# Rotating the query and key heads: the cosine product of the next vector ahead of the rest part of the one before

## The chip, the cores and the metric

The kernel runs on one core of a Trainium2 chip. The metric is the time of one execution on the device in microseconds (us). A core has five engines that work side by side: TensorE (PE in the profile, with its weight loads as PEld), VectorE (DVE), ScalarE (ACT), GpSimd (POOL) and SyncE (SP), which issues transfers. Each runs its own list of instructions in order and waits on semaphores that the others raise.

## The reference

A feed-forward part, attention and a second feed-forward part, each behind a layer norm and added to x. x has 4 sequences of 512 tokens of 256 values. In the attention, 16 query heads of 128 share 4 key heads. The part that the change touches is the rotation of queries and keys:

```python
def apply_rope(x):
    ...
    cos = jnp.cos(ang).astype(x.dtype)
    sin = jnp.sin(ang).astype(x.dtype)
    x1, x2 = (x[..., :half], x[..., half:])
    return jnp.concatenate([x1 * cos - x2 * sin, x1 * sin + x2 * cos], axis=-1)
...
q = apply_rope(q)
k = apply_rope(k)
...
scores = jnp.einsum('bhqd,bhkd->bhqk', q, k) * scale
causal = jnp.triu(jnp.ones((S, S), dtype=bool), k=1)
scores = jnp.where(causal, -jnp.inf, scores)
attn = jax.nn.softmax(scores, axis=-1)
out = jnp.einsum('bhqk,bhkd->bhqd', attn, v)
```

## The kernel before

**Steps.** The attention runs in 16 steps, one for each pair of key head and sequence. Each step has 4 query heads, so there are 5 vectors to rotate per step, r = 0 (the key) to 4, each 128 x 512 (128 values of a head in the partitions, 512 tokens). While step s computes its scores and outputs, the vectors of step s + 1 are projected and rotated. Steps 1 to 13 are a loop; step 0 is mixed with the end of the first feed-forward part, steps 14 and 15 are written out. Products are kept precise by splitting every operand into a leading part in fp32r and a rest, and multiplying three times.

**One vector's way.** TensorE projects it into the PSUM bank `pj`. ScalarE copies it into `raw[r]` (`raw_out`, L1528, raises `raw_done`). SyncE copies its two halves crosswise into `swap[r]` by two transfers. GpSimd then works on it in `rotate`: L1281 multiplies `raw[r]` by the cosine into `rot[r % 2]`, L1283 multiplies `swap[r]` by the sine, L1285 adds the two (raises `sum_done`). ScalarE copies the sum in fp32r to `qh` or, for r = 0, to the keys (`rotated_lead`, L1502, raises `qh_done`), and GpSimd subtracts that leading part from the sum (`rest`, L1273, raises `ql_done`). There are two buffers `rot`, so the cosine of vector r must come behind the rest of vector r - 2.

**ScalarE's order** in step s, for head h = 0 to 3: two copies of transposed probabilities (`prob_lead`, L1549), two exponentials (L1543), for h = 0 `raw_out(s + 1, 2)`, two more exponentials, for h = 1 and 2 `raw_out(s + 1, h + 2)`, for h = 3 `raw_out(s + 2, 0)` and `(s + 2, 1)`, for h = 0 `rotated_lead(s + 1, 0)` and `(s + 1, 1)` one behind the other, then the third `prob_lead`, the copy of the output (L1553), and for h > 0 `rotated_lead(s + 1, h + 1)`.

**Probabilities.** VectorE finds the row minima of the negated masked scores (L1386), ScalarE takes the exponentials and their sums, VectorE inverts the sums (L1391) and multiplies the probabilities by them in place (`normalise`, L1395): four TENSOR_SCALAR instructions of 128, 256, 384 and 512 columns, in SBUF. TensorE transposes the result (`transpose_p`, L1713). In step s, head h, TensorE computes the scores of the head after next, the transposes of the next head (eight, then two), and the output of head h (L1727 to L1729); in between stand the projections (L1648 to L1650) and the output projection of the step before (L1757 to L1759). The first of the eight transposes waits until all four L1395 of that head are done. L1395 runs one place ahead of the transposes that need it; a "head h" at which L1395 runs means the place h in the step.

At the entry GpSimd's list also has the last pieces of the first feed-forward part (`inverse_rms`, L315; `add_rows`, L320) and of the next layer norm (`rstd`, L1289); VectorE has the scaling of the last rows there (L570).

Of the kernel before, what the change touches and what calls it, by code (L numbers as in the profile page):

```python
# [1103 lines left out]
def attention(nc, sems, d, shared, banks, step_sems, passed, split, room):  # L1104
# [18 lines left out]
    with ExitStack() as ctx:  # L1123
# [34 lines left out]
        def qh(h):  # L1158
            return q_hi[h // 2][:, h % 2, :]

        def ql(h):
            return q_lo[h // 2][:, h % 2, :]
# [103 lines left out]
        def gpsimd(pool, tail):  # L1266
            inverse_rms, add_rows = tail

            def rest(s, r):
                pool.wait_ge(qh_done, NR * s + r + 1)  # L1270
                k = bass.ds(s % 2, 1)
                to, lead = (kl[:, k, :], kh[:, k, :]) if r == 0 else (ql(r - 1).unsqueeze(1), qh(r - 1).unsqueeze(1))
                pool.tensor_tensor(to, rot[r % 2][:].unsqueeze(1), lead.bitcast(F32), ALU.subtract).then_inc(ql_done, 1)  # L1273

            def rotate(s, r):
                if r >= 2:
                    pool.wait_ge(ql_done, NR * s + r - 1)
                elif not (isinstance(s, int) and s == 0):
                    pool.wait_ge(ql_done, NR * s)
                pool.wait_ge(raw_done, NR * s + r + 1)  # L1280
                pool.tensor_tensor(rot[r % 2][:], raw[r], cosT[:], ALU.mult)  # L1281
                pool.wait_ge(swap_in[r], 32 * s + 32)
                pool.tensor_tensor(swap[r], swap[r], sinT[:], ALU.mult).then_inc(sin_done, 1)  # L1283
                pool.wait_ge(sin_done, NR * s + r + 1)
                pool.tensor_tensor(rot[r % 2][:], rot[r % 2][:], swap[r], ALU.add).then_inc(sum_done, 1)  # L1285

            def rstd(k):
                pool.wait_ge(ln_var, k + 1)
                pool.tensor_tensor(rs[:, k], ve[:, k], mhalf[:], ALU.pow).then_inc(rstd_done, 1)  # L1289

            def rope(s):
                rotate(s, 0)
                for r in range(1, NR):
                    rest(s, r - 1)
                    rotate(s, r)

            last_block = BATCH - 1
            rotate(0, 0)
            add_rows(last_block - 1, 1)
            rest(0, 0)  # L1300
            rotate(0, 1)
            rest(0, 1)
            rotate(0, 2)
            inverse_rms(last_block, 0)
            rest(0, 2)
            rotate(0, 3)
            rest(0, 3)
            rotate(0, 4)
            inverse_rms(last_block, 1)
            add_rows(last_block, 0)  # L1310
            rest(0, 4)
            rotate(1, 0)
            rstd(0)
            rest(1, 0)
            rotate(1, 1)
            rstd(1)
            for r in range(2, NR):
                rest(1, r - 1)
                rotate(1, r)
            with pool.Fori(2, STEPS) as s:  # L1320
                rest(s - 1, NR - 1)
                rope(s)
            rest(STEPS - 1, NR - 1)
            rstd(2)
# [301 lines left out]
        def tensor(pe, tail, router):  # L1626
# [204 lines left out]
            output(STEPS - 1, range(G - 1, G))  # L1831

        return (wo, mask, mask_in, xu_done, rotated_lead, rows_normed), offsets, (sync, gpsimd, vector, scalar, tensor)


# [135 lines left out]
```

## Time and profile before

| | us |
|---|---|
| median of 3 runs | 825.73 (825.53 to 825.89) |
| the profiled execution | 827.23 |
| its span, first to last instruction | 825.4 |

| engine | busy us | share of the span |
|---|---|---|
| PE | 791.6 | 96% |
| PEld | 697.2 | 84% |
| DVE | 655.1 | 79% |
| POOL | 517.5 | 63% |
| ACT | 507.4 | 61% |

In the profile an engine's busy time is the time in which one of its instructions runs; register and semaphore instructions are not counted. A wait is put down to the instruction that raised the last semaphore. The chain of waits is followed back from the last instruction, at each step to what released it.

### The profile page before, as it was taken

The numbers are of one execution on the slowest core, as the hardware profiler recorded it, in microseconds if no ns is written. First come the engines' busy times: TensorE is split into PE (matmuls) and PEld (weight loads), VectorE is DVE, ScalarE is ACT, GpSimd is POOL, SyncE is SP. The second block draws the span as 40 slices with busy tenths as digits, with TensorE's granted clock in tenths as the row PEclk, the third lists the DMA queues.
The fourth block names the chain that finished last, engine by engine and source line by source line (L and its number), as shares of the span: only waits on it lengthen the run. The fifth ranks groups of instructions, "written<-read, shape, count | busy, mean of one in ns | idle before, by whom it ended". The sixth has DMA issues, their size and how long they took to land.

```text
span 825.4 us, 16046 instructions
## 1 busy us (share of the span) xinstructions
PE 791.6 (96%) x4712; PEld 697.2 (84%) x4712; DVE 655.1 (79%) x1917; ACT 507.4 (61%) x1250; POOL 517.5 (63%) x408
## 2 busy tenths in 40 slices
PE   7899999869999999999999999999999999999996
PEld 4688887758999989999899998999999988788885
DVE  6888996897678686786876868768687799988876
ACT  3555665657667576676865767557676586344543
POOL 4545739965878778777777777877878761112302
PEclk9999999979999999999999999999999999999998
DMA  9245321201132122212311313122131110000001
GB/s 290 82 144 191 120 85 39 66 13 39 27 77 76 38 51 76 51 27 62 105 28 45 93 30 80 29 85 51 35 92 25 39 27 1 1 1 26 2 26 52
DMA packets 28998, 50.09 MB, mean 61 GB/s; under 512 B 3874, under 2 KB 9634, under 8 KB 28962
## 3 DMA queue, kind: packets, MB, share of 16 engines
q1 hardware_dynamic: 28964, 49.67, 21.5%
q8 instruction: 17, 0.28, 0.1%
q14 instruction: 17, 0.14, 0.0%
HBM read 18.72 MB, written 9.96 MB: 35 GB/s over the span
## 4 chain that ended last, share of the span: by engine, by line
PE 80%; DVE 10%; ACT 3%; issue 2%; POOL 2%; DMA 1%; SPq 1%; POOLq 0%; DVEq 0%; ACTq 0%
PE pt L1713 8%; PE pj L1648 5%; PE pj L1650 5%; PE pj L1649 5%; PE o L1727 5%; PE o L1728 4%; PE o L1729 4%; PE sc L1702 4%; PE sc L1701 4%; PE sc L1700 4%; PE pj L1757 4%; PE pj L1758 3%; PE pj L1759 3%; PE sc L983 3%; PE sc L984 3%; PE sc L985 3%
## 5 line engine op out<-in xcount | busy, mean ns | idle before, releaser
L1273 POOL TENSOR_TENSOR at_ql<-at_rot,at_qh 128x512 fp32r<-128x512 f32 x64 | 82.6, 1291 | 100.5 <-ACT at_qh L1502 100.4
L1549 ACT ACTIVATE at_pth<-pt 128x512 fp32r<-128x512 f32 (+1 forms) x192 | 94.0, 524 | 82.4 <-PE pt L1713 82.4
L1400 DVE TENSOR_TENSOR at_ptl<-pt,at_pth 128x512 fp32r<-128x512 f32 (+1 forms) x192 | 108.9, 594 | 44.9 <-ACT at_pth L1549 44.7
L1543 ACT ACTIVATE at_pr<-at_pr,at_low 128x512 f32<-128x512 f32 (+3 forms) x256 | 140.5, 557 | 4.4 <-DVE at_low L1386 4.2
L1395 DVE TENSOR_SCALAR at_pr<-at_pr,at_inv 128x128 f32<-128x128 f32 (+3 forms) x256 | 107.6, 482 | 2.3
L1285 POOL TENSOR_TENSOR at_rot<-at_rot,gc 128x512 f32<-128x512 f32 x80 | 103.3, 1291 | 6.3
L1281 POOL TENSOR_TENSOR at_rot<-ga,cos 128x512 f32<-128x512 f32 x80 | 103.9, 1298 | 2.4 <-POOL at_ql L1273 2.3
L1283 POOL TENSOR_TENSOR gc<-gc,sin 128x512 f32<-128x512 f32 x80 | 103.7, 1296 | 1.0 <-DMA gc<-ga 1.0
L1713 PE MATMUL pt<-ident,at_pr 128*128 128x128 f32 x640 | 93.5, 277 | 8.3 <-DVE at_ptl L1400 4.6
L1386 DVE CUSTOM_DVE_ANT_0 at_pr<-sc,at_mask 128x512 f32<-128x512 f32 (+2 forms) x192 | 100.7, 548 | 0.2
L1502 ACT ACTIVATE at_qh<-at_rot 128x512 fp32r<-128x512 f32 x64 | 40.6, 634 | 91.1 <-POOL at_rot L1285 91.1
L1727 PE MATMUL o<-at_pth,at_vh 128*128 128x512 f32 (+3 forms) x256 | 83.1, 325 | 0.1
L1728 PE MATMUL o<-at_ptl,at_vh 128*128 128x512 f32 (+3 forms) x256 | 82.7, 323 | 0.0
L1729 PE MATMUL o<-at_pth,at_vl 128*128 128x512 f32 (+3 forms) x256 | 82.4, 322 | 0.0
L1713 PEld LDWEIGHTS pt<-ident,at_pr 128*128 128x128 f32 x640 | 70.8, 142 | 11.4 <-DVE at_ptl L1400 5.5
L1702 PE MATMUL sc<-at_keys,at_ql 128*128 (+4 forms) x256 | 76.8, 311 | 0.0
L1757 PE MATMUL pj<-at_wo,at_oh 128*128 128x256 f32 x248 | 71.7, 289 | 0.0
L734 ACT ACTIVATE sc<-sc 128x512 f32<-128x512 f32 x76 | 44.3, 583 | 43.2 <-PE sc L985 43.1
L1700 PE MATMUL sc<-at_keys,at_qh 128*128 (+3 forms) x192 | 70.3, 366 | 0.0
L1758 PE MATMUL pj<-at_wo,at_oh 128*128 128x256 f32 x248 | 70.1, 283 | 0.0
L1759 PE MATMUL pj<-at_wo,at_ol 128*128 128x256 f32 x248 | 70.1, 283 | 0.0
L498 DVE SCALAR_TENSOR_TENSOR f_acc<-sc,full,f_acc 128x256 f32<-128x256 f32 x130 | 56.5, 475 | 14.6 <-ACT sc L734 14.2
(286 smaller groups left out, 2265.2 us busy)
## 6 DMA issues: line engine op xcount, KB each, us to landing
gc<-ga SPq DMA_DIRECT2D x160, 128.0 KB, 2.3
ga<-in_attn_w SPq DMA_DIRECT2D x8, 384.0 KB, 4.9
gb<-attn_split SPq DMA_DIRECT2D x6, 512.0 KB, 4.1
at_wo<-attn_split SPq DMA_DIRECT2D x6, 512.0 KB, 4.0
attn_split<-gb SPq DMA_DIRECT2D x6, 384.0 KB, 2.4
attn_split<-gc SPq DMA_DIRECT2D x6, 384.0 KB, 3.3
x<-in_x SPq DMA_DIRECT2D x4, 512.0 KB, 9.5
e_raw<-in_expert_w SPq DMA_DIRECT2D x8, 256.0 KB, 6.6
```

The lines of the kernel that those rows point to most:

```text
L1281: pool.tensor_tensor(rot[r % 2][:], raw[r], cosT[:], ALU.mult)
L1283: pool.tensor_tensor(swap[r], swap[r], sinT[:], ALU.mult).then_inc(sin_done, 1)
L1395: dve.tensor_scalar(a, a, inv[h % 2][:, i:i + 1], None, ALU.mult).then_inc(nm_done, 1)
L1400: dve.tensor_tensor(ptl[h % 2][:, cols], pt[(NF * h + k) % 2][:, 0:FLEN[k]], pth[h % 2][:, cols].bitcast(F32), ALU.subtract).then_inc(lo_d ...
L1543: act.activation(pr[h % 2][:, cols], pr[h % 2][:, cols], ACT.Exp, bias=low[h % 2][:, i:i + 1], scale=-1.0, accum_out=tot[h % 2][:, i:i + 1 ...
L1700: pe.matmul(o, qh(h)[:, q], k_hi, start=True, stop=False)
L1702: r = pe.matmul(o, ql(h)[:, q], k_hi, start=False, stop=True)
L1713: r = pe.transpose(pt[(NF * h + k) % 2][:, col + (i - kt) * P:col + (i - kt + 1) * P], pr[h % 2][:, OFF[i] + kt * P:OFF[i] + (kt + 1) * P] ...
L1727: pe.matmul(o, vh[:, kt, :], pth[h % 2][:, a], start=(kt == 0), stop=False)
L1728: pe.matmul(o, vh[:, kt, :], ptl[h % 2][:, a], start=False, stop=False)
L1729: r = pe.matmul(o, vl[:, kt, :], pth[h % 2][:, a], start=False, stop=end)
L1757: pe.matmul(o, hi[:, tok], wo[0][:, h, :], start=(h == heads[0]), stop=False)
```

## The change

`rotate` is cut in two: `cosine` has the waits for the buffer and for the raw copy and the product L1281, `sine` has the rest. In `rope`, and in the order written out by hand for steps 0 and 1, the cosine of vector r is placed ahead of the rest of vector r - 1 instead of behind it, for r = 1 to 4. For r = 0 the order stays. Every instruction, operand and semaphore is the same, and the other engines' lists are untouched.

```diff
-            def rotate(s, r):
+            def cosine(s, r):
                 if r >= 2:
                     pool.wait_ge(ql_done, NR * s + r - 1)
...
                 pool.wait_ge(raw_done, NR * s + r + 1)
                 pool.tensor_tensor(rot[r % 2][:], raw[r], cosT[:], ALU.mult)
+
+            def sine(s, r):
                 pool.wait_ge(swap_in[r], 32 * s + 32)
                 pool.tensor_tensor(swap[r], swap[r], sinT[:], ALU.mult).then_inc(sin_done, 1)
...
             def rope(s):
-                rotate(s, 0)
+                cosine(s, 0)
+                sine(s, 0)
                 for r in range(1, NR):
+                    cosine(s, r)
                     rest(s, r - 1)
-                    rotate(s, r)
+                    sine(s, r)
...
-            rotate(1, 0)
+            cosine(1, 0)
+            sine(1, 0)
             rstd(0)
+            cosine(1, 1)
             rest(1, 0)
-            rotate(1, 1)
+            sine(1, 1)
             rstd(1)
             for r in range(2, NR):
+                cosine(1, r)
                 rest(1, r - 1)
-                rotate(1, r)
```

In the loop, GpSimd's list from the sum of vector 2 to the sum of vector 3 was this (`at_ql0` and `at_qh0` are the rest and leading part of the first two query heads, `ga` holds the raw copies, `gc` the swapped ones):

```order
L1285 TENSOR_TENSOR at_rot0<-at_rot0,gc 128x512 [waits at_sin_done]
L1273 TENSOR_TENSOR at_ql0<-at_rot0,at_qh0 128x512 [waits at_qh_done]
L1280 REGISTER_ALU [waits at_ql_done]
L1281 TENSOR_TENSOR at_rot1<-ga,cos 128x512 [waits raw_done]
L1283 TENSOR_TENSOR gc<-gc,sin 128x512 [waits swap_in3]
L1285 TENSOR_TENSOR at_rot1<-at_rot1,gc 128x512 [waits at_sin_done]
```

and is now this, with L1285 and L1287 for the sine and the sum:

```order
L1287 TENSOR_TENSOR at_rot0<-at_rot0,gc 128x512 [waits at_sin_done]
L1280 REGISTER_ALU [waits at_ql_done]
L1281 TENSOR_TENSOR at_rot1<-ga,cos 128x512 [waits raw_done]
L1273 TENSOR_TENSOR at_ql0<-at_rot0,at_qh0 128x512 [waits at_qh_done]
L1285 TENSOR_TENSOR gc<-gc,sin 128x512 [waits swap_in3]
L1287 TENSOR_TENSOR at_rot1<-at_rot1,gc 128x512 [waits at_sin_done]
```

The product by the cosine and its wait for the raw copy have moved ahead of the rest and its wait for ScalarE's leading part.

At the entry, in step 0, GpSimd's list around the rotation of the key and the first query of step 1 was this (`at_rs` is the inverse deviation of the next layer norm):

```order
L1285 TENSOR_TENSOR at_rot0<-at_rot0,gc 128x512 [waits at_sin_done]
L1289 TENSOR_TENSOR at_rs<-at_ve,mhalf 128x4 [waits at_ln_var]
L1273 TENSOR_TENSOR at_keys<-at_rot0,at_keys 128x512 [waits at_qh_done]
L1281 TENSOR_TENSOR at_rot1<-ga,cos 128x512 [waits raw_done,at_ql_done]
L1283 TENSOR_TENSOR gc<-gc,sin 128x512 [waits swap_in1]
```

and is now this, where L1291 is the former L1289:

```order
L1287 TENSOR_TENSOR at_rot0<-at_rot0,gc 128x512 [waits at_sin_done]
L1291 TENSOR_TENSOR at_rs<-at_ve,mhalf 128x4 [waits at_ln_var]
L1281 TENSOR_TENSOR at_rot1<-ga,cos 128x512 [waits raw_done,at_ql_done]
L1273 TENSOR_TENSOR at_keys<-at_rot0,at_keys 128x512 [waits at_qh_done]
L1285 TENSOR_TENSOR gc<-gc,sin 128x512 [waits swap_in1]
```

The product of the first query now stands between the inverse deviation and the rest of the key.

## Rows read from the trace of the kernel before

**Rows 1.** Stretches: each engine's busy us (instructions), one step; then granted clock, DMA.

```profile
400.12:434.01 33.89, 33.89 (x222) 31.02 (x221) 25.44 (x76) 22.83 (x60) 25.71 (x21) 1.00 0.26 70
```

**Rows 2.** Waits between 200 and 671 us: total us, times, longest us.

```profile
ACT at_qh L1502 <- POOL at_rot L1285: 81.2, 14, 5.8
...
PEld pj L1757 <- ACT ga L1528: 4.0, 13, 0.4
```

**Rows 3.** Chain of waits, 424 to 436 us: start us, us, what.

```profile
427.36 0.89 PE pt L1713 x8
...
433.52 1.03 PE pt L1713 x8
```

**Rows 4.** Timeline of GpSimd, 400 to 436 us: start us, us, instruction [idle before].

```profile
411.55 1.29 POOL L1285 TENSOR_TENSOR at_rot<-at_rot,gc 128x512 f32<-128x512 f32 x1
...
427.10 1.28 POOL L1273 TENSOR_TENSOR at_ql<-at_rot,at_qh 128x512 fp32r<-128x512 f32 x1 [1.79 <-ACT at_qh L1502]
...
430.97 1.29 POOL L1285 TENSOR_TENSOR at_rot<-at_rot,gc 128x512 f32<-128x512 f32 x1
```

**Rows 5.** Timeline of ScalarE, 400 to 436 us.

```profile
419.44 0.63 ACT L1502 ACTIVATE at_qh<-at_rot 128x512 fp32r<-128x512 f32 x1 [5.79 <-POOL at_rot L1285]
...
424.83 0.58 ACT L1528 ACTIVATE ga<-pj 128x512 f32<-128x512 f32 x1
...
431.00 0.58 ACT L1528 ACTIVATE ga<-pj 128x512 f32<-128x512 f32 x1
```

**Rows 6.** Timeline of VectorE, 400 to 436 us: L1395 in heads 3, 0, 1, 2.

```profile
403.74 1.84 DVE L1395 TENSOR_SCALAR at_pr<-at_pr,at_inv 128x128 f32<-128x128 f32 x4
...
413.13 1.27 DVE L1395 TENSOR_SCALAR at_pr<-at_pr,at_inv 128x128 f32<-128x128 f32 x4
...
425.17 1.28 DVE L1395 TENSOR_SCALAR at_pr<-at_pr,at_inv 128x128 f32<-128x128 f32 x4
...
431.35 1.97 DVE L1395 TENSOR_SCALAR at_pr<-at_pr,at_inv 128x128 f32<-128x128 f32 x4
```

**Rows 7.** Timeline of TensorE's weight loads, from 400 us, in four stretches.

```profile
407.53 0.85 PEld L1713 LDWEIGHTS pt<-ident,at_pr 128*128 128x128 f32 x8
...
420.98 0.85 PEld L1713 LDWEIGHTS pt<-ident,at_pr 128*128 128x128 f32 x8
...
427.15 0.86 PEld L1713 LDWEIGHTS pt<-ident,at_pr 128*128 128x128 f32 x8
...
433.45 0.86 PEld L1713 LDWEIGHTS pt<-ident,at_pr 128*128 128x128 f32 x8
```

**Rows 8.** Timeline of VectorE, first L1395 at 431.35 alone.

```profile
431.35 0.98 DVE L1395 TENSOR_SCALAR at_pr<-at_pr,at_inv 128x128 f32<-128x128 f32 x1
```

**Rows 9.** Timelines of single instructions, VectorE and GpSimd, near 167 and 414 us.

```profile
167.56 0.35 DVE L1395 TENSOR_SCALAR at_pr<-at_pr,at_inv 128x256 f32<-128x256 f32 x1
...
167.71 1.33 POOL L1273 TENSOR_TENSOR at_keys<-at_rot,at_keys 128x512 fp32r<-128x512 f32 x1 [1.69 <-ACT at_keys L1502]
...
167.83 1.43 DVE L1395 TENSOR_SCALAR at_pr<-at_pr,at_inv 128x384 f32<-128x384 f32 x1
...
413.93 0.48 DVE L1395 TENSOR_SCALAR at_pr<-at_pr,at_inv 128x512 f32<-128x512 f32 x1
...
413.95 1.60 POOL L1273 TENSOR_TENSOR at_keys<-at_rot,at_keys 128x512 f32 x1 [1.11 <-ACT at_keys L1502]
```

**Rows 10.** Timelines of VectorE and TensorE at the entry and behind the loop.

```profile
148.57 3.44 DVE L1395 TENSOR_SCALAR at_pr<-at_pr,at_inv 128x128 f32<-128x128 f32 x4
...
171.99 1.48 DVE L570 SCALAR_TENSOR_TENSOR f_y<-f_y,rr,rows 128x256 f32<-128x256 f32 x1
...
174.58 1.11 PE L1713 MATMUL pt<-ident,at_pr 128*128 128x128 f32 x4 [3.21 <-DVE at_ptl L1400]
...
674.91 1.90 DVE L1395 TENSOR_SCALAR at_pr<-at_pr,at_inv 128x128 f32<-128x128 f32 x4
```

**Rows 11.** Stretches, as in rows 1, at the entry.

```profile
172.00:176.00 4.00, 1.42 (x6) 1.32 (x7) 3.97 (x8) 1.38 (x3) 1.18 (x1) 0.59 0.00 0
```

More of the change, by code:

```diff
@@ L1291, in rope @@
             def rope(s):
-                rotate(s, 0)
+                cosine(s, 0)
+                sine(s, 0)
                 for r in range(1, NR):
+                    cosine(s, r)
                     rest(s, r - 1)
-                    rotate(s, r)
+                    sine(s, r)
             last_block = BATCH - 1
-            rotate(0, 0)
+            cosine(0, 0)
+            sine(0, 0)
             add_rows(last_block - 1, 1)
+            cosine(0, 1)
             rest(0, 0)
-            rotate(0, 1)
+            sine(0, 1)
+            cosine(0, 2)
             rest(0, 1)
-            rotate(0, 2)
+            sine(0, 2)
             inverse_rms(last_block, 0)
+            cosine(0, 3)
             rest(0, 2)
-            rotate(0, 3)
+            sine(0, 3)
+            cosine(0, 4)
             rest(0, 3)
-            rotate(0, 4)
+            sine(0, 4)
             inverse_rms(last_block, 1)
@@ L1311, in gpsimd @@
             rest(0, 4)
-            rotate(1, 0)
+            cosine(1, 0)
+            sine(1, 0)
             rstd(0)
+            cosine(1, 1)
             rest(1, 0)
-            rotate(1, 1)
+            sine(1, 1)
             rstd(1)
             for r in range(2, NR):
+                cosine(1, r)
                 rest(1, r - 1)
-                rotate(1, r)
+                sine(1, r)
             with pool.Fori(2, STEPS) as s:
```

## The prediction

> **What bounds the kernel now.** I read the stretches first. One step of the attention loop takes 33.89 us, and in it TensorE is busy from end to end at full granted clock, while VectorE has 25.4 us of work and GpSimd 25.7 [rows 1]. The chain of waits agrees: for the whole loop it runs along TensorE's matrix products. So whatever GpSimd or ScalarE gains inside a step is worth nothing by itself, and whatever makes TensorE wait costs its full length, once per step. The waits name the stall that the change shortens: ScalarE stands 14 times, 81.2 us in all, for GpSimd's sum [rows 2]; once per step, up to 5.8 us, at 419.44 [rows 5]. But it is nobody's bound: TensorE does not wait meanwhile.
>
> Next I looked for the places where TensorE has no reserve. Each head's probabilities are multiplied on VectorE by L1395 (four instructions), and eight transposes, L1713, wait for them. The weight loads of these transposes start at 420.98, 427.15 and 433.45 [rows 7]; the four products end at 414.41, 426.45 and 433.32 [rows 6]. At 433.45 TensorE is released 0.13 us after the product's end, so that is the latency of this hand-over, and the group takes 1.03 us in the chain instead of the 0.89 of the one at 427.36 [rows 3]: TensorE already waits 0.14 us there. There are 13 such pieces, one per step. The reserves are therefore 420.98 - 414.41 - 0.13 = 6.4 us (head 0 of the step), 427.15 - 426.45 - 0.13 = 0.57 us (head 1), and -0.14 (head 2). Head 3 has 407.53 - 405.58 - 0.13 = 1.8 us [rows 6, 7].
>
> **L1395 and GpSimd exclude each other.** With GpSimd idle the four products take 1.27 or 1.28 us, as at 413.13 and 425.17 [rows 6]. At 431.35 they take 1.97, since GpSimd's sum runs until 432.26 [rows 4] and the first product ends only at 432.33, 0.98 us long in place of 0.29 [rows 8]. The nearest thing to what the change makes is at 167: GpSimd starts 0.35 us after the first product; the second product still ends in its usual 0.35 us, the third starts at 167.83 and lasts 1.43 us, until 0.22 us after GpSimd's instruction ends at 169.04 [rows 9]. It goes by who begins first: at 413.93 the fourth product began 0.02 us before GpSimd's instruction, kept its 0.48 us, and GpSimd's was stretched to 1.60 [rows 9]. The Trainium skill (SBUF — State Buffer, Who interferes with whom) states the same for a fast-mode tensor_scalar, an exclusive lock for one whole instruction; it is the rule that speaks against this change, and by it the first rival below cannot be.
>
> **The change, part by part.** No instruction, transfer or wait is added; one product with the cosine (1.29 us, 1.25 start to start) moves ahead of a subtraction, four times per step. What moves is when GpSimd is busy, and what its queue stands behind: the cosine waits for ScalarE's raw copy L1528, and behind it the subtraction. ScalarE's order makes each raw copy come before the rotated copy that the subtraction waits for, so no wait is lengthened and nothing can lock.
>
> *Head 0.* The sum of 411.55 ends at 412.84 [rows 4] and the cosine now follows at once, as its raw copy is long done. The first product, ready at 413.13, waits until 414.1. From then on GpSimd has work without a pause (subtraction, sine, sum: 1.3 us each), so one product passes per GpSimd instruction, as the 1.43 us one in [rows 9] shows: the four end at about 418.4 instead of 414.41. The reserve of 6.4 us covers this 4.0. ScalarE's stall falls from 5.8 to about 4.5 us, and nothing waits for it. Cost 0, and 0 gain.
>
> *Head 1.* The raw copy starts at 424.83 [rows 5], takes 0.58 and is seen 0.08 later: the cosine starts at 425.49, for GpSimd has finished its previous sum by about 423.4 and would stand idle until 427.10 [rows 4]. The products start at 425.17 as before (ScalarE's exponentials release them). So GpSimd comes 0.32 us after the first product, as at 167: two products pass, the third waits until 426.85 and ends at 427.07, the fourth runs from 426.99 to 427.47. That is 2.30 us for the four instead of 1.28, +1.02. Of it 0.57 is reserve: **0.45 us of TensorE waiting.** If the interference cost nothing it would be 0; if the following subtraction (ready at 427.10, 0.11 us after the fourth product's start) got in first, 1.3 more. I take 0.45 by the nearest row. For the instruction itself the Trainium skill (Perfetto Trace Analysis, GPSIMD Engine Instruction) says not to trust GpSimd's spans but the spacing of their starts; by that, 1.25 in place of 1.29, the sum of this and the next term would be 1.0 us smaller. The first product's end 0.08 us after the recorded end at 432.26 speaks for the recorded one.
>
> *Head 2.* Everything is later by the 0.45. The products start at 431.80, the raw copy (431.00 [rows 5]) gives the cosine at 432.11, again 0.31 after. They end at 434.10; in the old frame 433.65 against 433.32. The old overlap with the sum (0.7 us) is gone, since that sum now ends 1.0 us earlier, and a larger one has come. **TensorE waits 0.33 us more** (0.47 in place of 0.14). The subtraction is ready 0.1 us after the fourth product starts, as before.
>
> *Head 3.* The sum no longer touches the products: 0.6 us faster, hidden behind 1.8 us of reserve.
>
> So a step takes 33.89 + 0.78 = 34.67 us. The loop has 13 steps: 13 x 0.45 = 5.9 and 13 x 0.33 = 4.3 us. The step after the loop has both costs (0.45 and 0.32, rounded), and there TensorE does wait in head 3 for the products at 674.91, 1.90 us long [rows 10]; without the sum they take 1.27: -0.6. Together +0.15.
>
> *Entry* (before 200 us). Head 0 of the first step: the four products at 148.57 take 3.44 us between GpSimd's instructions [rows 10]. By the new order GpSimd's sine comes 0.8 us earlier and ends at 149.25, with a cosine and a subtraction behind the sum; the four would end at 152.3 instead of 152.0: +0.3, between 0 and a whole further instruction (+1.4). At 171.99 the second L570 is held for 1.48 us by the sum [rows 10]. With the cosine done ahead, in GpSimd's idle 1.7 us before 167.71, the sum ends near 171.75 and the second L570 takes 0.48: -1.0; TensorE at 174.58 waits for VectorE right behind it (3.21 us idle) [rows 10]. TensorE's granted clock is 0.59 on average between 172 and 176 [rows 11], after its idle time; with idle stretches moved by a microsecond this may come, go or shift, and from the granted share I bound it at 2 us either way. Entry: -0.7, between -4 and +3.
>
> **Sum.** 5.9 + 4.3 + 0.15 - 0.7 = +9.6 us on the span of 825.4, so 835.0. The profiled execution took 827.23, which is 1.8 more than its span and 1.5 more than the median of 825.73; the forecast for the median is 825.73 + 9.6 = **835.3 us**, 1.2% slower.
>
> **Rivals.**
> 1. *VectorE keeps the port through its four products, and GpSimd waits.* Then only the relief counts: 13 x 0.14 at head 2, 0.6 behind the loop, 1.0 at the entry: -3.4, 822.3 us. This ends on the other side. For it: at 413.93 VectorE did come first. Against it: at 167.83 the port was lost between two products. It decides at the third product of head 1. Chance 0.08.
> 2. *The delay is absorbed,* by TensorE's wait of 0.3 us per step for L1528 [rows 2] or by products that start earlier; entry and end cancel: 825 +- 1. Against it: that wait hangs on ScalarE, which follows TensorE's transposes and so moves with them. Chance 0.06.
> 3. *Only one of the two places is hit,* if the cosine starts 0.3 us later than worked out at the other: -4.3 or -5.9, 829.5 to 831. Chance 0.08.
> 4. *The fourth product is lost too,* to the subtraction 0.1 us behind: 1.3 us more per place, 14 x 1.3 = 18 us for one place, 36 for both: 853 to 871. At 413.93 a lead of 0.02 us was enough for VectorE, so 0.06.
>
> The forecast has the rest, 0.72. Slower by over 0.2% (what a measurement of this kernel can tell from no change) is 0.72 + 0.08 + 0.06 = 0.86, within 0.06, faster 0.08. The forecast's own bounds are 9.6 - 5 and + 6 from the entry and from the 1.0 us of the spacing; with rival 3 the range is 829 to 841 and holds 0.80.
>
> **What the profile would show.** A step of 34.67 us; TensorE's weight loads L1713 with a wait for VectorE of about 0.45 and 0.47 us in heads 1 and 2; the four L1395 at 2.3 us there, some 5.2 in head 0 and 1.27 in head 3; ScalarE's wait for the sum 4.5 us in place of 5.8. I am wrong if L1395 keeps 1.3 us in head 1 while a cosine stands in GpSimd's row beside it, or if the third product is not the long one.

## The result

The changed kernel takes **835.71 us** (median of 4 runs, 833.99 to 838.05); the kernel before, 825.81 (4 runs, 825.53 to 825.91). The ratio is 1.012, with a 95% interval of 1.0107 to 1.0133: 9.9 us slower, where 835.3 was forecast.

The profiled execution of the change took 836.0 us, with a span of 833.8. That is 8.4 more than the span shown of before, and not 9.9. The profiled execution of before had been 1.5 us above its own median; how much of such a difference is TensorE's granted clock is taken up further down.

The page of the changed kernel: the busy times, and the costliest group of instructions in it.

```profile
PE 794.3 (95%) x4712; PEld 697.0 (84%) x4712; DVE 716.5 (86%) x1917; ACT 509.4 (61%) x1250; POOL 527.0 (63%) x408
...
L1407 DVE TENSOR_SCALAR at_pr<-at_pr,at_inv 128x128 f32<-128x128 f32 (+3 forms) x256 | 174.9, 744 | 2.3
```

VectorE is busy for 61 us more than before with the same instructions, and all of it looks like work. L1407, the former L1395, is now the costliest group of the page, with 174.9 us instead of 107.6. An instruction that is held up by another engine doesn't stand as idle time in this profile: it stands as busy time, and only its own duration tells. (The total doesn't say what the delay costs either: some 50 us of the 67 are head 0's, 3.9 us in each of 13 steps, and TensorE never waits for them.)

One step of the loop (columns as in [rows 1]: stretch, length, busy us of PE, PEld, DVE, ACT, POOL, granted clock, DMA):

```profile
392.35:427.05 34.70, 34.15 (x222) 31.08 (x221) 29.99 (x76) 22.96 (x61) 26.40 (x20) 1.00 0.26 68
```

A step takes 34.70 us instead of 33.89 [rows 1]. TensorE has the same 222 instructions at full granted clock, and for the first time stands idle in the step, 0.55 us by this row. The row doesn't show the whole wait: it also counts 34.15 us as busy where a step without any wait has 33.75 (the kernel with short cosines, below). The waits between 200 and 680 us (total, times, longest), as in [rows 2]:

```profile
ACT at_qh L1514 <- POOL at_rot L1287: 61.7, 14, 4.5
...
PEld pt L1725 <- issue: 10.9, 26, 0.4
PE pt L1725 <- DVE at_pr L1407: 7.5, 28, 0.3
```

The stall that the order shortens has shrunk from 5.8 to 4.5 us at the longest and from 81.2 to 61.7 in all. That is worth nothing, as nobody waited for ScalarE there. The last two rows are new: TensorE waits, at its weight loads and its products, for L1407. No such row was there in the loop of before, whose wait of 0.14 us showed only in the chain [rows 3]. That chain, 424 to 440 us (start us, us, what), now leaves TensorE:

```profile
427.05 1.42 DVE at_pr L1407 x3
...
428.89 0.48 DVE at_pr L1407
429.37 0.13 issue
...
432.37 1.08 ACT at_pr L1555 x5
...
433.69 1.41 DVE at_pr L1407 x3
...
436.13 1.09 PE pt L1725 x8
```

Twice per step, in heads 1 and 2, the end is now set by VectorE's products and the 0.13 us of the hand-over. Between the two places the chain runs over ScalarE's exponentials (L1555, the former L1543), not over TensorE's products: a head's delay reaches the next head through ScalarE, as the prediction had it ("Everything is later by the 0.45"). What stands beside them, VectorE first, then GpSimd and TensorE's weight loads, from the timelines between 415 and 445 us (start us, us, instruction, idle before it), heads 0, 1, 2, 3 for VectorE:

```profile
415.02 5.18 DVE L1407 TENSOR_SCALAR at_pr<-at_pr,at_inv 128x128 f32<-128x128 f32 x4
...
427.05 2.31 DVE L1407 TENSOR_SCALAR at_pr<-at_pr,at_inv 128x128 f32<-128x128 f32 x4
...
433.69 2.31 DVE L1407 TENSOR_SCALAR at_pr<-at_pr,at_inv 128x128 f32<-128x128 f32 x4
...
440.33 1.27 DVE L1407 TENSOR_SCALAR at_pr<-at_pr,at_inv 128x128 f32<-128x128 f32 x4
...
427.36 1.39 POOL L1281 TENSOR_TENSOR at_rot<-ga,cos 128x512 f32<-128x512 f32 x1 [2.13 <-ACT ga L1540]
428.96 1.53 POOL L1273 TENSOR_TENSOR at_ql<-at_rot,at_qh 128x512 fp32r<-128x512 f32 x1 [0.22 <-ACT at_qh L1514]
...
422.85 0.85 PEld L1725 LDWEIGHTS pt<-ident,at_pr 128*128 128x128 f32 x8
...
436.13 0.86 PEld L1725 LDWEIGHTS pt<-ident,at_pr 128*128 128x128 f32 x8 [0.42 <-issue]
```

And VectorE's third and fourth products of head 1 alone:

```profile
427.51 1.45 DVE L1407 TENSOR_SCALAR at_pr<-at_pr,at_inv 128x384 f32<-128x384 f32 x1
...
428.89 0.47 DVE L1407 TENSOR_SCALAR at_pr<-at_pr,at_inv 128x512 f32<-128x512 f32 x1
```

GpSimd's cosine starts at 427.36, 0.31 us after VectorE's first product, while the second is running. The third, queued for 427.51, is through only at 428.96 instead of some 427.93: it ends 0.21 us after GpSimd's instruction does at 428.75. The fourth starts at 428.89, 0.07 us ahead of GpSimd's subtraction at 428.96, and it keeps its 0.47 us, while the subtraction takes 1.53. In head 0 GpSimd works without a pause, one product passes per GpSimd instruction, and the four take 5.18 us; but they end at 420.20, and TensorE's weight loads come at 422.85 without a wait.

### The profile page after: what moved, and what is told of

It reads as the page before. It is cut to its first block, busy times and chain, and to the rows that moved or that the text cites. A ratio compares the mean times of both kernels' runs of the same rounds, so it can differ in the third digit from the quotient of the medians.

```text
span 833.8 us, 16046 instructions
## 1 busy us (share of the span) xinstructions
PE 794.3 (95%) x4712; PEld 697.0 (84%) x4712; DVE 716.5 (86%) x1917; ACT 509.4 (61%) x1250; POOL 527.0 (63%) x408
## 4 chain that ended last, share of the span: by engine, by line
PE 64%; DVE 16%; ACT 9%; issue 8%; POOL 2%; DMA 1%; ACTq 0%; DVEq 0%; SPq 0%; POOLq 0%
DVE at_pr L1407 7%; PE pt L1725 6%; ACT at_pr L1555 6%; PE pj L1769 4%; PE pj L1771 3%; PE pj L1770 3%; PE sc L983 3%; PE sc L985 3%; PE sc L984 3%; PE pj L1660 3%; PE pj L1662 3%; PE pj L1661 3%; PE sc L1714 2%; PE o L1739 2%; PE o L1740 2%
## 5 line engine op out<-in xcount | busy, mean ns | idle before, releaser
L1407 DVE TENSOR_SCALAR at_pr<-at_pr,at_inv 128x128 f32<-128x128 f32 (+3 forms) x256 | 174.9, 744 | 2.3
L1555 ACT ACTIVATE at_pr<-at_pr,at_low 128x512 f32<-128x512 f32 (+3 forms) x256 | 140.5, 557 | 5.5 <-DVE at_low L1398 5.4
L1281 POOL TENSOR_TENSOR at_rot<-ga,cos 128x512 f32<-128x512 f32 x80 | 109.0, 1362 | 46.1 <-ACT ga L1540 43.8
L1273 POOL TENSOR_TENSOR at_ql<-at_rot,at_qh 128x512 fp32r<-128x512 f32 x64 | 89.9, 1404 | 70.8 <-ACT at_qh L1514 70.8
L1287 POOL TENSOR_TENSOR at_rot<-at_rot,gc 128x512 f32<-128x512 f32 x80 | 104.0, 1299 | 6.3
L1285 POOL TENSOR_TENSOR gc<-gc,sin 128x512 f32<-128x512 f32 x80 | 104.4, 1305 | 1.1 <-DMA gc<-ga 1.0
L498 DVE SCALAR_TENSOR_TENSOR f_acc<-sc,full,f_acc 128x256 f32<-128x256 f32 x130 | 56.4, 475 | 13.2 <-ACT sc L734 12.8
```

Of the source, the lines that this page charges most:

```text
L1407: dve.tensor_scalar(a, a, inv[h % 2][:, i:i + 1], None, ALU.mult).then_inc(nm_done, 1)
L1555: act.activation(pr[h % 2][:, cols], pr[h % 2][:, cols], ACT.Exp, bias=low[h % 2][:, i:i + 1], scale=-1.0, accum_out=tot[h % 2][:, i:i + 1 ...
```

## The experiments

The theory: the cosine, placed ahead of the rest, falls on VectorE's products and holds up the third one, in heads 1 and 2, each time for 0.45 us of TensorE's time. The rivals: the loss comes from the entry or from another order on the other engines; it is one place only; or the order is bad in itself. The length of a step in the table is the mean of 11 steps of the loop, from the products of one head to those of the same head 11 steps later, from VectorE's timeline:

| kernel | step, us | time, us | ratio to before (95%) |
|---|---|---|---|
| before | 33.90 | 826.32; 826.13 | 1 |
| the change | 34.70 | 835.71 | 1.0120 (1.0107 to 1.0133) |
| the loop alone changed | 34.70 | 836.83 | 1.0129 (1.0099 to 1.0160) |
| the entry alone changed | 33.90 | 825.22 | 0.9986 (0.9974 to 0.9997) |
| the cosines of heads 1 and 2 short | 33.76 | 821.83 | 0.9941 (0.9921 to 0.9962) |
| vector 3 alone ahead | 34.23 | 831.16 | 1.0054 (1.0034 to 1.0073) |
| vector 4 alone ahead | 38.40 | 886.60 | 1.0722 (1.0680 to 1.0764) |
| the change, products with accumulator | 34.00 | 825.38 | 0.9981 (0.9965 to 0.9997) |
| the cosines behind the products | 33.76 | 822.43 | 0.9945 (0.9924 to 0.9967) |
| the same, and step 0's products with accumulator | 33.76 | 819.76 | 0.9922 (0.9897 to 0.9947) |

The change was timed against a before of 825.81. The first of the two times of before belongs to the loop alone, the short cosines, vector 4 and the first kernel with accumulator; the second to the other four.

**The loop alone, and the entry alone.** In the first, steps 2 to 16 get the new order and the order written out for steps 0 and 1 stays as before; in the second it is the other way round, and the loop's `rope` is written as before. At each place of the entry the edit is this one:

```diff
-            cosine(0, 1)
             rest(0, 0)
+            cosine(0, 1)
```

> The cosines are placed ahead in the loop and for the vectors of the later steps only; the entry (steps 0 and 1 of the rotation) keeps the order of before. Theory (VectorE's products L1407 lose the port to the cosine in heads 1 and 2): 34.7 us per step, as in the changed kernel, 14 steps with 0.8 each, less 0.6 behind the loop: about 10.5 us slower than before, near 836.3. Rival (a good part of the loss comes from the entry, or from TensorE's clock there): well under 8 us slower.

> The new order at the entry (steps 0 and 1 of the rotation) alone; the loop as before. Theory (the loss is the loop's): 33.89 us per step as before, the second L570 no longer held by the sum (1.0 us), less what the first products lose (0.2 us), and 0 to 1 us by TensorE's clock: 1 to 2 us faster than before, near 825.0 if before is at 826.3. Rival (the entry is a loss too): above before.

The loop alone gives 836.83 us, 10.5 above the before of its set (8.2 to 13.2 by the interval); the entry alone 825.22, 0.9 below (0.2 to 2.1). Their sum is 9.6, and the whole change measured 9.9. So the loss is the loop's, and the entry gives a little back.

**The cosines of heads 1 and 2 short.** The order is that of the change; in the loop the cosine of vectors 3 and 4 covers only 8 of the 512 columns, so those columns of the rotated queries, and the output, are not what the reference has.

```diff
+                n = SEQ if isinstance(s, int) or r < 3 else 8
-                pool.tensor_tensor(rot[r % 2][:], raw[r], cosT[:], ALU.mult)
+                pool.tensor_tensor(rot[r % 2][:, 0:n], raw[r][:, 0:n], cosT[:, 0:n], ALU.mult)
```

> The changed kernel, but in the loop the cosine product of vectors 3 and 4 takes 8 of the 512 columns, so that part of the rotation is left out; order, waits and queue are the same. Theory (it is the time for which the cosine holds the port): L1407 takes 1.3 us in heads 1 and 2, no wait of TensorE for it, 33.75 us per step, and in all 3 to 4 us faster than before, near 822. Rival (GpSimd's queue stands at the wait for the raw copy, and what is behind it comes late): still 34.7 us per step and near 835.

This takes the suspected overlap away and leaves every wait and every place in the queues; it also frees GpSimd a microsecond earlier each time. The timelines of VectorE and GpSimd of this kernel, head 1, then its whole step:

```profile
421.26 1.28 DVE L1408 TENSOR_SCALAR at_pr<-at_pr,at_inv 128x128 f32<-128x128 f32 x4
...
421.57 0.29 POOL L1282 TENSOR_TENSOR at_rot<-ga,cos 128x8 f32<-128x8 f32 x1 [2.13 <-ACT ga L1541]
...
387.51:421.26 33.75, 33.75 (x222) 30.98 (x221) 27.92 (x76) 22.95 (x61) 23.83 (x20) 1.00 0.26 70
```

The cosine starts as before 0.31 us after the first product, but it is over before the third needs to start, and the four take 1.28 us. TensorE is busy again from end to end. A step takes 33.76 us: the 0.14 us of before are gone with the sum that caused them, and both new waits too. This is the step without any wait, and it gives the prices: before waits 0.14 us per step, the change 0.94.

**One vector alone.** The new order for vector 3 only (its cosine falls on head 1), or for vector 4 only (head 2); the rest of the loop and the entry are as before.

```diff
             for r in range(1, NR):
-                cosine(s, r)
-                rest(s, r - 1)
+                if r in (3,):
+                    cosine(s, r)
+                    rest(s, r - 1)
+                else:
+                    rest(s, r - 1)
+                    cosine(s, r)
                 sine(s, r)
```

> Entry as before; in the loop the cosine of vector 3 alone is ahead (head 1). Theory: head 1 as in the changed kernel, 2.3 us for the four products and 0.4 to 0.45 us of waiting; in head 2 the sum of vector 3 has ended 0.6 us before the products, which then take 1.27 us, so TensorE's old wait of 0.14 us goes: +0.3 us per step, 34.2, and about 4.3 us in all, near 830. Rival (the two heads' losses hang together and one alone costs nothing, or as much as both): 826 or 836.

> Entry as before; in the loop the cosine of vector 4 alone is placed ahead (head 2), all others behind the rest as before. Theory (one product passes between two instructions of GpSimd, since the sum of vector 3, the cosine of 4 and the rest of 3 now stand in a row without a pause): in head 2 L1395's four products last some 5 us in place of 1.97, and TensorE waits about 3 us per step: 36.9 us per step, near 866 in all. Rival (the two places cost what they cost in the changed kernel, each by itself): +0.3 to 0.4 us per step, near 831.

Vector 3 alone behaves as worked out. The products of heads 1 and 2 in its timeline of VectorE:

```profile
425.80 2.31 DVE L1411 TENSOR_SCALAR at_pr<-at_pr,at_inv 128x128 f32<-128x128 f32 x4
432.44 1.27 DVE L1411 TENSOR_SCALAR at_pr<-at_pr,at_inv 128x128 f32<-128x128 f32 x4
```

Head 1 has the whole cost and head 2 none, since the earlier sum no longer reaches it. A step takes 34.23 us, 0.47 more than the one without a wait; that is the price of one place, and two places are the 0.94 of the change.

Vector 4 alone isn't the other half: it is 60 us slower than before. GpSimd is then still at the previous sum when the products of head 2 start, and has three more instructions ready. Timelines of VectorE, GpSimd and TensorE, head 2:

```profile
456.70 5.04 DVE L1411 TENSOR_SCALAR at_pr<-at_pr,at_inv 128x128 f32<-128x128 f32 x4
...
456.32 1.28 POOL L1287 TENSOR_TENSOR at_rot<-at_rot,gc 128x512 f32<-128x512 f32 x1
457.56 1.30 POOL L1281 TENSOR_TENSOR at_rot<-ga,cos 128x512 f32<-128x512 f32 x1
458.81 1.32 POOL L1273 TENSOR_TENSOR at_ql<-at_rot,at_qh 128x512 fp32r<-128x512 f32 x1
460.09 1.37 POOL L1285 TENSOR_TENSOR gc<-gc,sin 128x512 f32<-128x512 f32 x1
...
461.88 1.09 PE L1729 MATMUL pt<-ident,at_pr 128*128 128x128 f32 x8 [3.01 <-DVE at_pr L1411]
```

One product passes between two instructions of GpSimd, and all four are held. The expectation had this, and 866 us with it; measured were 886.60 (885.23 and 887.98, 2 runs). The stretches show the other 20 us (two steps one behind the other, then two parts of the step ahead of them, around the end of TensorE's idle time):

```profile
456.70:493.67 36.97, 33.96 (x222) 31.03 (x221) 27.98 (x75) 22.84 (x61) 25.88 (x21) 1.00 0.24 64
493.67:533.48 39.81, 36.80 (x222) 33.30 (x221) 27.98 (x75) 23.08 (x61) 25.90 (x21) 0.91 0.14 33
...
422.90:423.60 0.70, 0.00 (x0) 0.00 (x0) 0.70 (x2) 0.00 (x0) 0.62 (x2) 0.54 1.05 404
423.00:427.00 4.00, 3.38 (x14) 3.07 (x14) 4.00 (x14) 1.98 (x5) 1.53 (x2) 0.58 0.40 156
```

Where the granted clock stays at 1.00 a step takes 36.98 us from head 2 to head 2, as expected. In three steps of four it doesn't: late in TensorE's idle time of some 3 us the clock falls (0.54 on average between 422.90 and 423.60, when TensorE has done nothing since 420.6) and stays low for a few microseconds (0.58 between 423 and 427, so mostly the lower level of 1.2 GHz). These steps take 38.3, 38.6 and 39.8 us, and the mean of all is 38.40. So the time is made of 3.2 us of waiting and 1.4 us of lower clock per step. In the idle time that ended at 461.88, of the same length, it didn't fall. What decides which of them has a fall wasn't tested.

**Products in another form.** The change, with L1407 written so that the instruction also writes a sum of its result into `low`, which is free by then:

```diff
-                    dve.tensor_scalar(a, a, inv[h % 2][:, i:i + 1], None, ALU.mult).then_inc(nm_done, 1)
+                    dve.tensor_scalar(a, a, inv[h % 2][:, i:i + 1], 0.0, ALU.mult, ALU.add, accum_out=low[h % 2][:, i:i + 1]).then_inc(nm_done, 1)
```

> The changed kernel, with L1407 written as a TENSOR_SCALAR that also sums its row into an unused place; the products are the same. Theory (the products and GpSimd exclude each other only in the fast form; with the sum of the row, as L1398 shows, 512 columns take 0.61 us from start to start and GpSimd is not in the way): the four take about 1.7 us in every head, whatever GpSimd does; under the reserve of head 1 and less than 1.97 in head 2, so 33.75 us per step; at the entry, where the four took 2.3 to 4.2 us, 3 to 5 us less on the path. About 819, faster than both. Rival (they exclude each other in every form, or the loss has to do with the order of GpSimd's instructions): 34.7 us per step or more, and 835 or more.

If GpSimd holds up these products because both want something that only one can have, a form that doesn't want it must be free of it, with GpSimd's list untouched. The timelines of VectorE and GpSimd, head 1:

```profile
420.28 0.35 DVE L1407 TENSOR_SCALAR_CACHE_REDUCE at_pr<-at_pr,at_inv 128x128 f32<-128x128 f32 x1
...
420.55 0.48 DVE L1407 TENSOR_SCALAR_CACHE_REDUCE at_pr<-at_pr,at_inv 128x256 f32<-128x256 f32 x1
...
420.95 0.61 DVE L1407 TENSOR_SCALAR_CACHE_REDUCE at_pr<-at_pr,at_inv 128x384 f32<-128x384 f32 x1
...
421.49 0.75 DVE L1407 TENSOR_SCALAR_CACHE_REDUCE at_pr<-at_pr,at_inv 128x512 f32<-128x512 f32 x1
...
420.59 1.30 POOL L1281 TENSOR_TENSOR at_rot<-ga,cos 128x512 f32<-128x512 f32 x1 [2.38 <-ACT ga L1540]
```

The cosine runs beside the products from 420.59 to 421.89, and none of them is held: the third takes 0.61 us. The Trainium skill (SBUF — State Buffer, Who interferes with whom) says that a tensor_scalar can take the ports that it shares with GpSimd, except in the form that also writes out its accumulator. This case agrees, with 0.61 against 1.45 us for the third product at the same distance from the cosine. The price was underestimated, however: the four take 1.96 us (420.28 to 422.24) instead of 1.27, which is 0.69 more, and 0.57 is reserve, so TensorE still waits some 0.12 us in heads 1 and 2, and a step takes 34.00 us. It was expected at 819 us and is at 825.38: the change's loss is gone, but no more. Of the 6.4 us that are missing, 13 times 0.24, or 3.1, are the steps; the rest lies outside of them and wasn't followed up.

**The cosines behind the products.** In the loop, for vectors 3 and 4, GpSimd waits until the head's four products are done, and then takes the cosine ahead of the rest; for vectors 1 and 2 the order is that of before:

```diff
-                cosine(s, r)
-                rest(s, r - 1)
+                if r in (3, 4):
+                    pool.wait_ge(nm_done, BT * (G * (s - 1) + r + 1))
+                    cosine(s, r)
+                    rest(s, r - 1)
+                else:
+                    rest(s, r - 1)
+                    cosine(s, r)
```

> The changed kernel, but in the loop the cosines of vectors 1 and 2 stand behind the rest as before, and those of 3 and 4 wait until VectorE has done the four products of that head, and then go ahead of the rest. Theory (the place is right, the moment is wrong): in head 1 the products take 1.27 us; in head 2 the sum of vector 3 ends 0.5 us earlier than before, the products take 1.4 to 1.5 us in place of 1.97, and TensorE does not wait: 33.75 us per step, 2 us less than before in the loop, 1 to 2 at the entry: 822 to 823. Rival (GpSimd's later rest and sum, 0.7 us behind, now are late for ScalarE or TensorE): 34 us per step or more.

Timelines of VectorE, heads 1 to 3, and of GpSimd, head 1:

```profile
421.16 1.27 DVE L1412 TENSOR_SCALAR at_pr<-at_pr,at_inv 128x128 f32<-128x128 f32 x4
427.33 1.50 DVE L1412 TENSOR_SCALAR at_pr<-at_pr,at_inv 128x128 f32<-128x128 f32 x4
433.50 1.75 DVE L1412 TENSOR_SCALAR at_pr<-at_pr,at_inv 128x128 f32<-128x128 f32 x4
...
422.59 1.28 POOL L1281 TENSOR_TENSOR at_rot<-ga,cos 128x512 f32<-128x512 f32 x1 [1.26 <-DVE at_pr L1412]
423.84 1.30 POOL L1273 TENSOR_TENSOR at_ql<-at_rot,at_qh 128x512 fp32r<-128x512 f32 x1
```

GpSimd stands still for 1.26 us in head 1 and 1.23 in head 2, nearly all of it by the added wait, and the kernel gets faster than before: 822.43 us, with the step of 33.76 that has no wait. The cosine still comes ahead of the rest. So it isn't the order that costs, but where the instruction falls: for these two vectors the order is that of the change, and with the wait the kernel is 3.7 us below its before, without it 9.9 above. (Vectors 1 and 2 have the old order here; in the new one GpSimd's list is dense during the products of head 0, which the short-cosine kernel left at 5.18 us, with the same step of 33.76.)

**The same, with the accumulator form in step 0.** There GpSimd's list is dense and the products of head 0 have no other way out:

```diff
+                    if isinstance(n, int) and n < 4:
+                        dve.tensor_scalar(a, a, inv[h % 2][:, i:i + 1], 0.0, ALU.mult, ALU.add, accum_out=low[h % 2][:, i:i + 1]).then_inc(nm_done, 1)
+                    else:
+                        dve.tensor_scalar(a, a, inv[h % 2][:, i:i + 1], None, ALU.mult).then_inc(nm_done, 1)
```

> The kernel of e7 with the products of the first four heads (n = 0 to 3, the entry) in the form that also sums its row. Theory: at the entry the four take 2.0 us in place of 2.3 to 4.2 where GpSimd is busy; by the trace of e4 TensorE stands 2.4 us further ahead at 200 us than in the changed kernel: 2 to 2.5 us faster than e7, 820 to 821. Rival (VectorE's products are not what the entry waits for): as e7.

It takes 819.76 us, the fastest version here, 0.8% below before. The first four products take some 2.0 us; without this form they take 3.76 (3.44 in the kernel before [rows 10]). By the traces TensorE is 0.6 us ahead of the kernel without the form already at 140 us, before any of these products; it is 1.3 ahead at 150 and 1.9 at 172, so 0.7 and 1.3 of that can be the form's. The intervals of the last two kernels overlap (0.9924 to 0.9967, 0.9897 to 0.9947), so the step between them, 2.7 us by the medians, isn't shown as firmly as that both beat the kernel before.

## Why the prediction was right

**Head 1.** Forecast: four products of 2.30 us, the third the long one, 0.45 us of waiting. Measured: 2.31, 1.45 for the third, and 0.47 of waiting (vector 3 alone, 34.23 - 33.76). The reading of one odd place at 167 us [rows 9] carried over to within hundredths of a microsecond, since the cosine came at the same distance from the first product.

**Head 2.** Forecast: 2.30 us and 0.47 of waiting instead of 0.14. Measured: 2.31, and 0.94 - 0.47 = 0.47. The old wait of 0.14 is confirmed by the step of 33.76 that has neither.

**Head 3 and head 0.** 1.27 and 5.18 us, forecast 1.27 and some 5.2. Of head 0's reserve of 6.4 us the delay took 3.9; 422.85 - 420.20 - 0.13 = 2.5 are left. ScalarE's stall went to 4.5, as forecast.

**The step and the loop.** 34.70 - 33.90 = 0.80 against 0.78. The whole loop, with the two heads of the step behind it, moves TensorE by 11.1 us (from 2.88 ahead of before at 193 to 8.23 behind at 671), and the products behind the loop, now 1.27 us, give 0.6 back. That is 10.5, against 5.9 + 4.3 + 0.15 = 10.35; the loop alone measured 10.5 as a time.

**The entry.** This is the term that the profile doesn't confirm as it stands: forecast was -0.7, and the traces differ by 2.9 us at 193 us. Three things are in it. The second L570, alone in VectorE's timeline of the change, takes 0.47 us instead of 1.48, as forecast, and TensorE behind it starts 1.93 us earlier than before (172.65 for 174.58 [rows 10]), of which it had 1.2 already at 150 us:

```profile
171.07 0.47 DVE L570 SCALAR_TENSOR_TENSOR f_y<-f_y,rr,rows 128x256 f32<-128x256 f32 x1
...
172.65 1.11 PE L1725 MATMUL pt<-ident,at_pr 128*128 128x128 f32 x4 [2.20 <-DVE at_ptl L1412]
```

The first products take 3.75 us instead of 3.44, +0.3, as forecast. The rest is the clock, in stretches of before that the change doesn't have, first before and then change, columns as in [rows 11]:

```profile
32.00:36.00 4.00, 4.00 (x12) 3.10 (x13) 3.13 (x7) 1.33 (x2) 2.21 (x3) 0.60 0.00 0
...
180.00:188.00 8.00, 6.22 (x37) 5.70 (x35) 7.81 (x19) 5.21 (x12) 7.06 (x7) 0.79 0.14 33
```

```profile
32.00:36.00 4.00, 3.84 (x16) 3.04 (x17) 3.46 (x9) 1.92 (x3) 2.73 (x3) 1.00 0.00 0
...
180.00:188.00 8.00, 6.49 (x40) 5.75 (x41) 7.95 (x19) 6.32 (x17) 6.74 (x5) 1.00 0.13 29
```

Between 32 and 36 us nothing of the change runs yet, and still TensorE is 1.2 us ahead from there on. None of the other kernels profiled has this low stretch, so it belongs to the one execution of before that was profiled. The stretch from 180 to 188 us is another matter. It goes with the old order of the entry: each of the four kernels profiled with that order has a low stretch there or a little later (vector 4 alone at 191 us), and none of the six with the new one has. First the loop alone, then the entry alone:

```profile
180.00:188.00 8.00, 6.51 (x33) 5.98 (x34) 7.83 (x19) 5.45 (x12) 6.99 (x6) 0.79 0.15 34
180.00:188.00 8.00, 6.40 (x39) 5.66 (x40) 7.95 (x19) 6.33 (x16) 6.75 (x6) 1.00 0.14 32
```

Counted from 40 us, past the stretch of the one execution, TensorE gains 1.7 us on before until 193 us in the change and in the entry alone, and nothing in the loop alone. That is the 0.7 of the sum and 1.0 more that came with the granted clock, inside the 2 us that I had set aside for it. By medians of many runs, the entry is worth 0.9 us (the entry alone, 0.2 to 2.1); the other way to it, 10.5 of the loop alone less the 9.9 of the whole change, gives 0.6, but the interval of the first alone is 5 us wide, so it decides nothing. How often an execution has the low stretch with either order isn't known, and so the difference between 1.7 and 0.9 stays open.

**The range.** Its bounds of -5 and +6 around 9.6 are wider than the terms named for them: the entry (-4 to +3 around -0.7) and the 1.0 us of the spacing give -4.3 and +3.7. The 1.0 us wasn't needed: waits of 0.47 each agree with the recorded lengths of GpSimd's instructions, and not with the shorter spacing of their starts.

**The rivals.** VectorE didn't keep its place through four products: the third was held. The delay wasn't absorbed: ScalarE's raw copies came later with TensorE, as the prediction had it. Both places were hit, at 0.31 us each. The fourth product escaped the subtraction by 0.07 us, where 0.1 was forecast. That the margin had the right sign was luck; once there, it held in step after step, with 2.31 us for the four in heads 1 and 2 throughout the loop. The chance of 0.06 for it was rather low for so small a margin.

## What to carry to other kernels

Before an instruction is moved on a GpSimd that is no bound, look at what it will run beside on VectorE, not only at who waits for its result: here a stall shortened by 1.3 us was worth nothing, and an overlap of 1.3 us cost 0.47 us, twice per step. The step's length without the overlap comes cheaply, by making the suspected instruction short and leaving the order alone. And where two engines exclude each other, a wait that lets the engine off the path stand until the critical one is through can be worth more than the order: here it took a step to 33.76 us, below the 33.90 and 34.70 of the two orders without it.

## What the runs showed of the hardware that was not expected

- Between two GpSimd instructions that follow without a pause one of these VectorE products passes, whatever its length. The four took 5.04 and 5.18 us (1.27 alone). A lead of 0.07 us decided for a whole instruction.
- Not every VectorE instruction is held. In the kernel before, L1386, which reads the scores from PSUM, took 0.68 us in the midst of GpSimd's subtraction of 427.10 [rows 4], and none of the loop's L1386 took over 0.69. Timeline of VectorE:

```profile
427.30 0.68 DVE L1386 CUSTOM_DVE_ANT_0 at_pr<-sc,at_mask 128x512 f32<-128x512 f32 x1
```

- Idle time of some 3 us per step on TensorE cost more than itself: in the kernel with vector 4 alone, the granted clock fell in three of four of these idle times, 1.4 us per step on top of 3.2. The 0.4 us gaps of the change had no such effect: the clock was 1.00 in its steps.
- The product with accumulator took 0.35, 0.48, 0.61 and 0.75 us for 128 to 512 columns; without it they take 0.29, 0.35, 0.41 and 0.48. It escapes GpSimd, but isn't free.
